# Due times in an attention pipeline: a late scaling, an accumulator copy, statistics, weight bits and the first probability banks are moved

## The reference

```
x = x + layernorm(attention(layernorm(x)))
x = x + layernorm(ffn(layernorm(x)))

attention: q = rms_norm(x wq^T) * q_norm_w   (32 heads of 64)
           k = rms_norm(x wk^T) * k_norm_w,  v = x wv^T   (8 heads of 64, each for 4 query heads)
           scores = q k^T / 8 + slope[h] * (s - t), allowed where -256 <= s - t <= 0
           out = softmax(scores) v, then out wo^T
ffn:       h = silu((x gate_w^T) * gate_s) * ((x up_w^T) * up_s);  (h down_w^T) * down_s   (1408 wide)
```

## Time and profile before

| | us |
|---|---|
| median of 3 runs | 1207.07 (1206.99 to 1207.17) |
| the profiled execution, its own time | 1205.83 |
| its span | 1204.1 |
| TensorE matmul busy | 1163.0 (97%) |
| VectorE busy | 896.2 (74%) |
| ScalarE busy | 745.7 (62%) |
| GpSimd busy | 304.9 (25%) |
| mean granted TensorE clock | 0.997 |

### The profile page before, as it was taken

One profiled execution on the slowest core, in us unless ns is written; L12 is line 12 of the kernel. 1 busy time (PEld: TensorE's weight loads), 2 busy tenths in 40 slices (PEclk: granted clock), 3 DMA queues, 4 the chain that ended last, 5 costly groups with the idle time before them and its releaser, 6 DMA issues.

```text
span 1204.1 us, 26656 instructions
## 1 busy us (share of the span) xinstructions
PE 1163.0 (97%) x9016; PEld 990.8 (82%) x9016; DVE 896.2 (74%) x2328; ACT 745.7 (62%) x1582; POOL 304.9 (25%) x353
## 2 busy tenths in 40 slices
PE   7999999999999999999999999999999999999997
PEld 5778888887778888888888898898888888888876
DVE  5587878687898888888888888888866575546464
ACT  4546555556999877777778788888862443222230
POOL 3000000001788733323333423233311100202022
PEclk9999999999999999999999999999999999999999
DMA  5316355347676756355645654557436440303020
GB/s 175 105 44 245 141 215 204 140 193 257 222 235 221 249 178 232 124 188 195 205 148 169 214 190 153 170 179 214 141 95 227 147 130 30 105 1 105 1 70 36
DMA packets 100898, 189.55 MB, mean 157 GB/s; under 512 B 9376, under 2 KB 39072, under 8 KB 100768
## 3 DMA queue, kind: packets, MB, share of 16 engines
q1 hardware_dynamic: 100768, 187.88, 46.1%
HBM read 116.22 MB, written 71.63 MB: 156 GB/s over the span
## 4 chain that ended last, share of the span: by engine, by line
PE 91%; DVE 4%; ACT 2%; issue 2%; DMA 0%; POOL 0%; SPq 0%; DVEq 0%; POOLq 0%; ACTq 0%
PE bank L1408 21%; PE bank L1541 19%; PE bank L1473 15%; PE bank L1346 12%; PE bank L1434 12%; PE bank L1452 3%; PE bank L1450 3%; PE bank L1451 3%; PE bank L1462 2%; DVE pT_lo L1168 1%; PE bank L1518 1%; PE bank L1373 0%; DVE pT_lo L1172 0%; ACT y_raw L937 0%; PE bank L1363 0%
## 5 line engine op out<-in xcount | busy, mean ns | idle before, releaser
L802 ACT ACTIVATE p_sb<-u_sb,low 128x384 f32<-128x384 f32 (+2 forms) x512 | 271.9, 535 | 63.2 <-DVE low L1054 54.7
L1054 DVE CUSTOM_DVE_ANT_0 u_sb<-bank,bias 128x384 f32<-128x384 f32 (+2 forms) x512 | 229.3, 452 | 45.0 <-PE bank L1346 23.5
L1346 PE MATMUL bank<-k_st,q_st 128*128 128x384 f32 (+2 forms) x1024 | 252.4, 329 | 0.5 <-DVE low L1054 0.4
L1434 PE MATMUL bank<-ident,p_sb 128*128 128x128 f32 x1152 | 217.8, 280 | 23.8 <-DVE pT_lo L1168 13.0
L1168 DVE TENSOR_TENSOR pT_lo<-bank,pT_hi 128x384 f16<-128x384 f32 (+2 forms) x392 | 178.3, 455 | 37.1 <-ACT pT_hi L913 29.7
L1434 PEld LDWEIGHTS bank<-ident,p_sb 128*128 128x128 f32 x1152 | 139.2, 140 | 57.4 <-issue 25.1
L913 ACT ACTIVATE pT_hi<-bank 128x384 f16<-128x384 f32 (+2 forms) x392 | 159.6, 407 | 39.4 <-PE bank L1434 36.1
L1346 PEld LDWEIGHTS bank<-k_st,q_st 128*128 128x128 f32 x1024 | 169.3, 192 | 17.2 <-DVE low L1054 0.9
L696 POOL TENSOR_TENSOR o_out<-o_raw,inv_sum 128x256 f32<-128x256 f32 x128 | 80.3, 628 | 308.1 <-DVE inv_sum L1180 308.1
L1541 PE MATMUL bank<-zT_hi,gu 128*128 128x512 f32 x352 | 139.3, 396 | 0.6 <-DVE hid L1297 0.6
L1541 PE MATMUL bank<-zT_lo,gu 128*128 128x512 f32 x352 | 138.3, 393 | 0.0
(11 more groups left out here) (134 smaller groups left out, 2317.5 us busy)
## 6 DMA issues: line engine op xcount, KB each, us to landing
q_st<-q_scr SPq DMA_DIRECT2D x32, 1024.0 KB, 8.0
q_scr<-qk SPq DMA_DIRECT2D x61, 512.0 KB, 2.7
k_st<-k_scr SPq DMA_DIRECT2D x64, 256.0 KB, 3.3
o_scr<-o_out SPq DMA_DIRECT2D x128, 128.0 KB, 3.7
o_in<-o_scr SPq DMA_DIRECT2D x16, 768.0 KB, 5.6
z_in<-z_scr SPq DMA_DIRECT2D x8, 1024.0 KB, 6.2
k_scr<-qk SPq DMA_DIRECT2D x12, 512.0 KB, 2.7
v_scr<-v_out SPq DMA_DIRECT2D x4, 1040.0 KB, 6.5
```

Of the source, the lines that this page charges most:

```text
L802: nc.scalar.activation(p_sb[:, u % RING, 0:w], u_sb[:, u % RING, 0:w], ACT.Exp, scale=-1.0, bias=low[:, u % RING:u % RING + 1]).then_inc(p ...
L1054: nc.vector.tensor_tensor_reduce(out=u_sb[:, u % RING, 0:w], in0=bank[u % 2][:, 0:w], in1=bias[2 * u // UNITS][:, u % REP, at:at + w], sca ...
L1346: mm = nc.tensor.matmul(bank[u % 2][:, 0:w], q_st[:, s, r, P * i:P * i + P], k_st[:, s, part, P * key:P * key + w], start=(part == 0), sto ...
L1434: mm = nc.tensor.transpose(bank[probability_bank(A)][:, P * j:P * j + P], p_sb[:, u % RING, P * j:P * j + P], ident[:])
```

## The change

Four due times move, the twins end one pair earlier, and the bank pairs of the twins change turns, so that units 0 and 1 use banks 6 and 7. The wait for `v_out` moves to units 2 and 3, which now are the first in banks 2 and 3.

```
-TAKE_Y_AT, STATS_AT, NORM_AT = 1, 3, 6
+TAKE_Y_AT, STATS_AT, NORM_AT = 0, 2, 6
-TWINS = LAG * UNITS - 2 * TT
+TWINS = LAG * UNITS - 2 * TT - 2
-BITS_AT = (19, 20, 21)
+BITS_AT = (10, 19, 28)
-LATE_AT = {4: (2, 4, 18, 20), 3: (4, 18, 20), 1: (8,)}
+LATE_AT = {4: (2, 4, 18, 20), 3: (4, 18, 20), 1: (17,)}
@@ probability_bank
-    return unit % 2 + (6 if unit < TWINS and unit // 2 % 2 else 2)
+    return unit % 2 + (6 if unit < TWINS and unit // 2 % 2 == 0 else 2)
@@ transpose_p
-                if n == 0 and u < 2:
-                    pe.wait_ge(v_ready, TT * (B - 1) + 2 + u + 1)
+                if n == 0 and u in (2, 3):
+                    pe.wait_ge(v_ready, TT * (B - 1) + u + 1)
```

## The result

| | before | after |
|---|---|---|
| median, us | 1207.03 (1206.67 to 1207.17) | 1223.78 (1223.34 to 1227.1) |
| the profiled execution, own time | 1205.83 | 1223.98 |
| its span | 1204.1 | 1222.2 |
| TensorE matmul busy | 1163.0 (97%) | 1163.4 (95%) |
| mean granted TensorE clock | 0.997 | 0.995 |

The ratio is 1.0145, with the interval 1.0127 to 1.0163: slower, by 16.8 us where 9.7 were forecast.

A forecast was written before the change was run, and what follows sets the result against it. TensorE, with 91% of the chain that ended last, was taken as the bound. Late norm -14.2, first bits +23.8, count +0.6, copy and statistics -0.5 summed to +9.7, giving 1216.8 us; range 1208 to 1225.

The forecast's parts named there:

- five falls of the clock: Upper end of the range: TensorE's clock falling five times in the new holes, making 1216.8 + 8.4 = 1225.2 us.
- The late norm: Steps 4 to 10, from unit 8 to 17: saves 2.03 us a step, -14.2; colliding at 17 had chance 0.05.
- The first bits: Steps 4 to 14, gather moved to unit 10: VectorE waits for the third transfer, TensorE stalls 1.98 us each; +23.8 in all.
- `z_out` beside the gather: Unit 10: GpSimd's operation slows the gather by some 0.4 us in 5 steps, +2.0.
- The stall in sum: TensorE before unit 10's transposes, steps 4 to 14: 1.98 us a step plus 2.0 in all, together +23.8.
- The clock: TensorE: forecast kept its clock; a rival had it fall in the new holes, up to 1.7 us each, chance 0.12.
- Bits 2 and 3, and the count: Gathers at units 19 and 28 cost 0; the count at unit 10 in step 15 costs +0.6, bounds 0 to +1.1.
- Copy and statistics: Head of steps 5 to 15, accumulator copied at unit 0, statistics at 2: net -0.5 us, bounds -2.6 to +3.0.
- Banks, twins: Start of attention and seam of steps 3 and 4: each 0, bounds -1.1 to +0.3 and -1.0 to +0.5.
- The rival in which the bits hold nothing: Bits at unit 10 don't hold VectorE, or it is given back: 1193.0 us; needs a 2.2 us transfer; chance of faster 0.08.
- By steps: Attention: steps 4 to 10 stay near 40.8 us, steps 11 to 14 rise from 38.7 to about 40.9.

The follow-up runs named there:

- e3: The kernel before with only the late norm moved, from unit 8 to unit 17; 1193.57 us, ratio 0.9895.
- e9: The kernel before with only the late norm moved, by one unit from 8 to 9; 1195.37 us, ratio 0.9896.
- e2: The kernel before with only the weight bits moved, from units 19, 20, 21 to 10, 19, 28; 1223.94 us, ratio 1.0138.
- e4: The changed kernel with SP issuing the three loads of the bits first in the step, bits still at units 10, 19, 28; 1193.54 us, ratio 0.9892.
- e6: The changed kernel with the first gather of bits one unit later, at 11 instead of 10; 1205.11 us, ratio 0.9987.
- e12: The changed kernel with the first gather of bits three units later, at 13 instead of 10; 1192.87 us, ratio 0.9886.
- e1: The changed kernel with the weight bits back at units 19, 20 and 21, everything else changed; 1192.72 us, ratio 0.9883.

## Why the prediction came out as it did

The direction, the mechanism and the place were right; the size was 7 us short (8.4 in the profiled executions: 18.1 against 9.7). That 1223.8 lies inside 1208 to 1225 is partly luck: the upper end was drawn for five falls of the clock, and it was nearly reached with two falls and longer stalls.

- **The late norm** (forecast -14.2): right. e3 measures -13.5, and the scaling takes 0.75 at most. e9, with the scaling behind GpSimd's product, takes 1.8 of the 2.03 away, 1.07 of them as the scaling's own lengthening. The Trainium skill, GPSIMD Engine Reference (specifications), says that GpSimd shares its SBUF interfaces with VectorE and contends with VectorE's instructions that have two inputs in SBUF. The trace agrees: 1.82 us beside the product, 0.75 once it has ended (e9). At u = 17 the bound of 0 to 0.3 a step was the right one; 0.1 was paid.
- **The first bits** (forecast +23.8): the mechanism to the letter, 11 waits for the third transfer, 11 holes before the transposes of unit 10. The step that was mis-sized is "14.31 + 0.05 (semaphore) + 0.69". The third transfer took 4.37 us in the mean, not 4.0 (+0.37 a step), and up to 5.4. Part of that is this execution's: the mean is 4.08 in the kernel before and 3.9 to 4.2 in e2, e4, e6 and e12. From landing to the gather's start 0.16 us pass, not 0.05 (+0.11), so the estimate was too low. And in step 9 SP's first issue took 1.88 us instead of some 0.38 (+0.14 in the mean). The stall was forecast as 1.98; with these terms it is 2.60 before any sharing with GpSimd.
- **`z_out` beside the gather** (forecast +2.0 within the 23.8): the mechanism is there, the size isn't. Later landings put most gathers behind `z_out`; two of the 11 share with it and lose 0.5 us in all. Step 11 has one, GpSimd and VectorE:

```profile
717.63 1.27 POOL L725 TENSOR_TENSOR z_out<-y_n,x_res 128x512 f32<-128x512 f32 x1
...
718.39 1.05 DVE L1203 TENSOR_TENSOR used_bits<-used_bits,f_bits 128x512 int32<-128x512 int32 x1 [1.54 <-DMA f_bits<-downT]
```

- **The stall in sum**: by these terms 2.65 a step against 1.98 + 2.0/11 = 2.16. Measured, steps 4 to 14 of the kernel after are together 31.6 us longer than e1's, where 23.8 were forecast. Of the 31.6 the clock took 3.2 (below); the other 28.4 are 2.58 a step, 4.6 us above the forecast.
- **The clock**: the forecast kept it, and gave its fall a rival's chance of 0.12. In the profiled execution it fell twice, behind the two longest holes, 2 x 1.6 = 3.2 us. With the 4.6 that is 7.8 of the 8.4; the rest is small and spread, over the start of attention (+0.2), step 3 (+0.15) and what the late norm and the head left. That rival's picture of a fall, up to 1.7 us each, was right, its count of five too high; the forecast and the rival each hold a part of what happened. The Trainium skill, TensorE: Matmul & The Clock Gate (what's actually happening), says that an idle TensorE gets the lower clock. The trace now agrees inside attention as well, but the length of the hole alone does not decide here: holes of 2.65 and 2.90 (steps 5 and 10) brought no fall, in e2 holes of 2.40 and 2.15 did. What else decides is open.
- **Bits 2 and 3, and the count** (0 and +0.6): e12 has bits 2 and 3 at 19 and 28 and is level with e1, so 0 holds. Step 15 is 0.38 longer, within the bounds of 0 to 1.1.
- **Copy and statistics** (-0.5): the net is right, 0.08 to 0.10 a step earlier from unit 6 on, against 0.05 forecast. But I costed the copy at what TensorE's wait for it gave and charged "under 0.1" to ScalarE; I did not follow the chain ScalarE's rounding, split, split, through which the copy alone is worth 0.47 a step. The statistics at 2 hid that.
- **Banks, twins** (0, 0): right within 0.2. The hole at unit 1 goes and the one before unit 4 grows to 1.67; step 3 is 0.15 longer.
- **The rival in which the bits hold nothing**: it would have needed a third transfer of 2.0 us by the prediction's own sum (4.0 - 1.98), not 2.2; nothing hangs on it.
- **By steps**: 11 to 13 at 40.8 to 41.3, forecast 40.9; 4 to 10 at 41.67 in the mean, forecast 40.8. The difference there is the longer stall in seven steps and the fall in step 9.

## What to carry to other kernels

Before a wait is moved earlier in an in-order queue, compare the time at which its data stand, taken from the latest transfers and with the semaphore's part, with the time at which the engine arrives; a consumer is moved only together with its loads, since e4 buys back 30 us with two lines in SP's stream. When an operation is slow in one place only, look at what another engine does at that moment and move it away from that; one unit may do (e9). And judge the halves of a coupled edit apart: copy at 0 was worth 5 us, statistics at 2 gave 4 of them away.

## What the runs showed of the hardware

- VectorE's operations with two inputs in SBUF nearly stand still while a GpSimd operation runs that began before them: the gather takes 0.69 alone, 1.05 beside the tail of `z_out`, up to 1.69 beside the low part of 1.28 us (e2). Splits, one of whose inputs is a PSUM bank, kept their 0.55 to 0.56. Where VectorE's operation began first, it kept its time and GpSimd's became longer. In step 0 of the kernel before, GpSimd's product for `o_out`, which takes 0.61 alone, takes 0.93 beside a scaling of 0.72 that began 0.25 ahead of it. In these cases the one that began second loses the time of the overlap less 0.14 to 0.20 us; that the order of the starts decides is read from such pairs, no run changes it alone. Timelines of VectorE and GpSimd there:

```profile
311.19 0.72 DVE L1094 SCALAR_TENSOR_TENSOR raw_first<-raw_first,norm_w,inv_rms 128x512 f32<-128x512 f32 x1
...
311.44 0.93 POOL L696 TENSOR_TENSOR o_out<-o_raw,inv_sum 128x256 f32<-128x256 f32 x1 [3.50 <-DVE inv_sum L1180]
```

- A waiting VectorE instruction starts 0.16 us after its transfer has landed, in the mean of 11.
- SP's issues, mostly 0.32 to 0.43 us, now and then take much longer: 1.88 in step 9, 2.09 in step 7 of e6. What it waited for can't be seen in the profile.
- The granted clock fell to 0.50 at the end of some idle holes of TensorE of 2.15 to 3.36 us or up to 1.4 us behind it, and each fall cost about 1.6 us; behind others of 2.65 and 2.90 it did not. In e2 two such stretches (columns as above) were:

```profile
725.70:729.10 3.40, 3.40 (x13) 2.93 (x13) 1.68 (x4) 2.33 (x6) 0.00 (x0) 0.50 0.79 307
807.60:811.00 3.40, 3.17 (x25) 3.04 (x26) 2.05 (x7) 1.56 (x3) 0.00 (x0) 0.51 0.96 327
```
